# Splitting W_qkv's first two fifths inside the cross stage, and W_o with the first attention rows inside the self stage

## The reference

```python
x = x + cross_attention(layernorm(x), ctx_512)        # 16 heads over 1024 context rows
x = x + self_attention(layernorm(x))                  # w_qkv: 2560 x 512, 32 query heads, 4 key/value heads, causal
x = x + ffn(layernorm(x))                             # 16 experts, 4 chosen for a token, and a shared expert
...
qkv = jnp.einsum('bsh,oh->bso', hidden_states, w_qkv)
...
return jnp.einsum('bso,ho->bsh', out, w_o)            # w_o: 512 x 2048
```

## Time and profile before

| what | us |
|---|---|
| median of 3 runs | 1498.34 |
| lowest, highest | 1495.42, 1498.8 |
| the profiled execution | 1496.33 |
| its span, first to last instruction | 1494.4 |
| TensorE busy in it | 1355.5 |
| end of cross, start of self | 785 |
| end of self, start of MoE | 1059 |

### The profile page before, as it was taken

The page is one execution under the profiler, slowest core; times in us unless marked ns, Lnnn a source line. Parts: engine busy times, 40 slices in busy tenths (PEclk is TensorE's granted clock), DMA queues, the critical chain, the costliest instruction groups (busy, mean ns, idle before and its releaser), DMA issues. The chain is left out here.

```text
span 1494.4 us, 22780 instructions
## 1 busy us (share of the span) xinstructions
PE 1355.5 (91%) x7136; PEld 1109.7 (74%) x7136; DVE 800.7 (54%) x1371; ACT 737.9 (49%) x1741; POOL 573.0 (38%) x346
## 2 busy tenths in 40 slices
PE   5998699999999999999975999998689989999992
PEld 4776577878787878787854888887578768787772
DVE  4444366666666666666634445444479853432226
ACT  2444465565656565656524677777432214333331
POOL 2430133233332323232003333333346486427975
PEclk9999799999999999999997999999699999999997
DMA  5785414141414141413094111112643256536667
GB/s 195 262 269 178 172 50 149 54 173 50 175 49 175 48 177 43 182 42 113 1 330 178 64 64 50 50 50 99 225 146 132 78 184 225 174 121 224 233 201 232
DMA packets 78984, 209.79 MB, mean 140 GB/s; under 512 B 5888, under 2 KB 39168, under 8 KB 72960
## 3 DMA queue, kind: packets, MB, share of 16 engines
q1 hardware_dynamic: 69472, 163.78, 31.7%
q0 software_dynamic: 7136, 38.80, 7.6%
q10 hardware_dynamic: 2304, 6.29, 1.1%
HBM read 154.59 MB, written 92.01 MB: 165 GB/s over the span
## 5 line engine op out<-in xcount | busy, mean ns | idle before, releaser
L700 DVE TENSOR_TENSOR probsT_lo<-psTr,probsT_hi 128x512 fp32r<-128x512 f32 x256 | 176.7, 690 | 168.0 <-ACT probsT_hi L653 167.7
L653 ACT CAST probsT_hi<-psTr 128x512 fp32r<-128x512 f32 x256 | 150.1, 587 | 199.0 <-PE psTr L784 195.3
L784 PE MATMUL psTr<-ident,probs 128*128 128x128 f32 x1024 | 153.6, 274 | 11.3 <-DVE probsT_lo L700 5.2
L784 PEld LDWEIGHTS psTr<-ident,probs 128*128 128x128 f32 x1024 | 124.3, 141 | 50.4 <-DVE probsT_lo L700 13.5
L695 DVE TENSOR_REDUCE nmax<-psS 128x1 f32<-128x1024 f32 x128 | 155.5, 1215 | 9.5 <-PE psS L66 8.4
L610 ACT ACTIVATE probs<-psS,nmax 128x1024 f32<-128x1024 f32 x128 | 143.8, 1123 | 12.2 <-DVE nmax L695 12.2
L566 POOL TENSOR_TENSOR ctxT_lo<-ctx_f,ctxT_hi 128x512 fp32r<-128x512 f32 x32 | 41.4, 1295 | 278.0 <-ACT ctxT_hi L617 278.0
L64 PE MATMUL bank<-w_slots,ao_first_hi 128*128 (+1 forms) x252 | 108.5, 430 | 16.2 <-DVE w_slots L1807 9.6
L64 PE MATMUL psS<-kT_hi,qe 128*128 128x512 f32 x256 | 113.0, 441 | 3.7 <-DMA qe<-qe 2.8
L64 PE MATMUL psV<-probsT_hi,kv_hi 128*128 128x512 f32 x256 | 114.7, 448 | 0.6
L1513 POOL TENSOR_TENSOR w_slots<-w_ahead,w_slots 128x3072 fp32r<-128x3072 f32 x15 | 102.1, 6809 | 1.2
(11 more groups left out here) (273 smaller groups left out, 3323.8 us busy)
## 6 DMA issues: line engine op xcount, KB each, us to landing
w_ahead<-w_exp POOLq DMA_DIRECT2D x14, 1536.0 KB, 7.4
qe<-stage SPq DMA_DIRECT2D x16, 1024.0 KB, 6.8
qe<-qe SPq DMA_DIRECT2D x16, 1024.0 KB, 5.0
wraw<-w_pairs SPq DMA_DIRECT2D x8, 1792.0 KB, 11.5
early<-xs SPq DMA_DIRECT2D x47, 256.0 KB, 2.7
xs<-h_rows SPq DMA_DIRECT2D x47, 256.0 KB
early<-ctx SPq DMA_DIRECT2D x16, 512.0 KB, 11.6
ao<-attn_out SPq DMA_DIRECT2D x32, 256.0 KB, 2.4
```

The costliest lines, as they stand in the source:

```text
L653: act.copy(PT[k % PTN].hi[:], psT[slot][:]).then_inc(turned_hi, 1)
L700: dve.tensor_tensor(out, psT[slot][:], f32(hi), ALU.subtract).then_inc(turned_free, 1)
L784: last = pe.transpose(psT[slot][:, q * P:(q + 1) * P], src(q), ident[:])
```

## The change

**Memory.** One tensor `w_slots` is now allocated at the start for all blocks, and F, the queries, the keys, the context's parts, W_qkv, h2T, W_o and the first attention rows are views into it (`Shared`). Only by that can one block write into what the next one reads. Names in the lists change with it.

**In cross.** After its own work SyncE now also loads h2T for tiles 0 and 1, and, once a fifth is split, fifths 2 and 3 of W_qkv into the same two raw buffers. ScalarE casts fifth 0 after step k = 3 of the last half and fifth 1 after step k = 5 (`wqkv_high`), and waits there for the load; VectorE subtracts one step later (`wqkv_low`). The wait of ScalarE for the last two stores at the block's end is gone; it stands in later lists.

**In self.** The prologue has only fifths 2, 3 and 4 to split. W_o's quarters are loaded in units 2, 4, 6 and 7 of the first eight. In the last eight, GpSimd casts quarter c after its `norm` of unit c + 2, and VectorE subtracts it after its reciprocals of unit c + 3; in unit 6 GpSimd casts the first half of the attention rows, and in unit 7 VectorE subtracts them.

**In MoE.** The splits of W_o and of the first half-rows, the waits for them, and the load of the fourth quarter are gone. The second tile's first rows no longer wait for the first half of the projection.

```diff
+W_STEPS = (3, 5)
...
+        sp.wait_ge(pv_done, LT * (HB * NT - 1))
+        sp.wait_ge(h2_out, 16 * 3)
+        for j in range(2):
+            sp.dma_start(f32(HT[j]), h2_d[j].rearrange("p a x -> p (a x)")).then_inc(keep["ht_in"][j], 16)
+        for j in range(2):
+            sp.wait_ge(w_ready, j + 1)
+            sp.dma_start(keep["early"][j], t["w_qkv"][2 + j]).then_inc(w_in[2 + j], 16)
...
+        def wqkv_high(c):
+            act.wait_ge(s_mm, RT * HB * NT)
+            act.wait_ge(w_in[c], 16)
+            act.copy(W[c].hi, keep["early"][c]).then_inc(w_hi, 1)
...
+                    if not more and k in W_STEPS:
+                        wqkv_high(W_STEPS.index(k))
...
-        act.wait_ge(x1_out, 16 * NT + 16)
-        act.wait_ge(h2_out, 16 * NT + 16)
...
+        def wqkv_low(c):
+            dve.wait_ge(w_hi, c + 1)
+            dve.tensor_tensor(W[c].lo, keep["early"][c], f32(W[c].hi), ALU.subtract).then_inc(w_ready, 1)
...
+                    if not more and k - 1 in W_STEPS:
+                        wqkv_low(W_STEPS.index(k - 1))
...
+WO_SPLIT = (2, 3, 4, 5)
+WO_STEPS = (2, 4, 6, 7)
...
+            if isinstance(u, int) and u in WO_STEPS:
+                c = WO_STEPS.index(u)
+                if c == 0:
+                    sp.wait_ge(w_ready, WCH)
+                sp.dma_start(wo_raw[c], t["w_o"][:, c * KC:(c + 1) * KC, :]).then_inc(wo_in[c], 16)
...
+            if last and v in WO_SPLIT:
+                wo_high(WO_SPLIT.index(v))
+            if last and v == GI - 2:
+                pool.wait_ge(q_mm, NGRP)
+                pool.wait_ge(keep["a_in"][0], 16)
+                pool.tensor_copy(AS.hi, a_first).then_inc(wo_hi, 1)
...
-        high(0)
-        high(1)
+        high(2)
...
+            if last and v - 1 in WO_SPLIT:
+                c = WO_SPLIT.index(v - 1)
+                dve.wait_ge(wo_hi, c + 1)
+                dve.tensor_tensor(WO[c].lo, wo_raw[c], f32(WO[c].hi), ALU.subtract).then_inc(wo_lo, 1)
+            if last and v == GI - 1:
+                dve.wait_ge(wo_hi, HQ // 2 // KC + 1)
+                dve.tensor_tensor(AS.lo, a_first, f32(AS.hi), ALU.subtract).then_inc(wo_lo, 1)
...
-                if tt == 0 and h % KC == 0:
-                    pe.wait_ge(wo_lo, h // KC + 1)
```

More of the change, by code:

```diff
@@ L53 @@
 W_AHEAD = HQ * DH // P // KC - 1
+AT_QE, AT_KEYS = 0, 4 * H * S
+AT_F = AT_KEYS + 4 * L
+AT_KV = AT_F + 2 * H * D
+AT_CT = AT_KV + 4 * LT * DC
+WS_ALL = AT_CT + 2 * H * P
+WCH = 5
+WSZ = 2 * KC * BANK
+AT_A = 9 * KC * BANK
+HTZ, VBZ = 2 * KC * P, 8 * HKV * DH
+AT_CONST = WCH * WSZ
+AT_VB = AT_KV + 2 * HTZ
+AT_PT = AT_VB + 2 * VBZ
+assert AT_CONST + BANK + P <= AT_KV and AT_PT + 2 * REP * P <= WS_ALL
+assert 4 * W_B + 2 * T <= WS_ALL - AT_KV
 NE, TOPK, NG, TOPG, I = 16, 4, 4, 2, 256
@@ L77, in at, with __init__, shaped @@
         return self.hi[idx], self.lo[idx]
+class Shared(Pair):
+    def __init__(self, ws, at, dims):
+        n = int(np.prod(dims))
+        self.hi, self.lo = (shaped(ws[:, at + j * n:at + (j + 1) * n], dims) for j in range(2))
+def shaped(ap, dims):
+    names = "abcd"[:len(dims)]
+    return ap.rearrange(f"p ({' '.join(names)}) -> p {' '.join(names)}", **dict(zip(names, dims)))
 def f32(ap):
@@ L507, in tiles @@
         iteration(NT - 1, False, True)
+    W = [Shared(ws, c * WSZ, (KC, BANK)) for c in range(2)]
+    HT = [ws[:, AT_KV + j * HTZ:AT_KV + (j + 1) * HTZ] for j in range(2)]
+    w_in, w_hi, w_ready = keep["wqkv_in"], keep["wqkv_hi"], keep["wqkv_ready"]
     block = ctx.enter_context(nc.Block())
@@ L886, in sb @@
         return ctx.enter_context(nc.sbuf_tensor(name, shape, dt))
-    W = Pair(ctx, nc, "wqkv", [P, WCH, KC, BANK])
-    raw = keep["early"] + keep["ahead"][:WCH - 2]
+    ws = keep["ws"]
+    W = [Shared(ws, c * WSZ, (KC, BANK)) for c in range(WCH)]
+    a_first = keep["early_all"][:, 0:HQ // 4 * P].rearrange("p (h x) -> p h x", x=P)
+    raw = keep["early"] + keep["early"] + keep["ahead"][:1]
     tab = sb("rope_s_tab", [P, 2, 3, DH // 2])
-    mask_f, mask = sb("mask_f", [P, BANK]), sb("mask_r", [P, BANK], F32R)
-    ident_r = sb("ident_r", [P, P], F32R)
-    HT = [sb(f"h2T{j}", [P, 2, KC, P], F32R) for j in range(2)]
+    wo_raw = keep["ahead"] + [sb("wo_last", [P, KC, BANK])[:]]
+    WO = [Shared(ws, c * WSZ, (KC, D)) for c in range(HQ // 2 // KC)]
+    AS = Shared(ws, AT_A, (HQ // 4, P))
+    wo_hi, wo_lo = sem("wo_hi"), sem("wo_lo")
+    mask_f, mask = sb("mask_f", [P, BANK]), ws[:, AT_CONST:AT_CONST + BANK]
+    ident_r = ws[:, AT_CONST + BANK:AT_CONST + BANK + P]
+    HT = [shaped(ws[:, AT_KV + j * HTZ:AT_KV + (j + 1) * HTZ], (2, KC, P)) for j in range(2)]
     QR = sb("q_terms", [P, 2, BANK])
@@ L960, in _ @@
     def _(sp):
-        sp.dma_start(HT[0][:].bitcast(F32).rearrange("p a k x -> p a (k x)"), t["h2T"][0]).then_inc(ht_in[0], 16)
         sp.dma_start(tab[:], t["rope_s"]).then_inc(tab_in, 16)
         sp.dma_start(mask_f[:], t["mask"]).then_inc(tab_in, 16)
[L964 to L970, removed]
+        sp.dma_start(raw[4], t["w_qkv"][4]).then_inc(w_in[4], 16)
         def step(i, v, last):
             u, tt, g, ahead = plan(i, v, last)
+            if isinstance(u, int) and u in WO_STEPS:
[3 more added lines that the diff above has]
+                sp.dma_start(wo_raw[c], t["w_o"][:, c * KC:(c + 1) * KC, :]).then_inc(wo_in[c], 16)
             if last and v == 2:
@@ L1098, in step @@
                 exps(u + 1, (v + 1) % 2)
+            if isinstance(u, int) and u == 1:
+                act.wait_ge(keep["h2_out"], 16 * NT + 16)
             if not (isinstance(u, int) and u == 0):
@@ L1147, in v_low @@
                                       ALU.subtract).then_inc(v_lo, 1)
[L1149 to L1150 removed]
+        low(2)
         dve.wait_ge(tab_in, 32)
@@ L1153, in _ @@
         terms_q(0)
-        low(2)
+        low(3)
         terms_q(1)
-        low(3)
+        dve.wait_ge(keep["x1_out"], 16 * NT + 16)
         maxes(0, 0)
@@ L1331, in build_moe @@
     acc = sb("acc", [P, NT, D])
-    WS = sb("w_slots", [P, (NSLOT - 1) * SLOT + 2 * KC * T], F32R)
+    WS = keep["ws"]
     h3 = [WS[:, (NSLOT - 1) * SLOT + j * KC * T:(NSLOT - 1) * SLOT + (j + 1) * KC * T].rearrange(
```

110 lines of the change are left out of this document (52 added, 58 removed).

## The result

| what | before | after |
|---|---|---|
| median of 4 runs each, us | 1497.57 | 1515.04 |
| lowest, highest | 1495.42, 1498.8 | 1513.6, 1519.25 |
| the profiled execution | 1496.33 | 1515.2 |
| its span | 1494.4 | 1513.2 |

The ratio is 1.0117, its 95% interval 1.0099 to 1.0135: the change makes the kernel 17.5 us slower. The forecast was +19.1, and 1517.4 us counted from the median of 1498.34 that three runs had; a fourth has joined them.

What follows compares the result with a forecast made beforehand. TensorE, busy 91% of the span, was taken as the bound, so only its waits count. +19.2 (first keys) - 1.5 (prologue) + 1.4 (W_o) = +19.1 us, giving 1517.4 us; range 1507 to 1525, slower 93%.

Steps and rivals of the forecast that it cites:

- fifth 0 in the raw buffer, ScalarE's cast starts: End of cross: fifth 0 of W_qkv, queued behind 8 MB of fills, lands at 779 (776 to 781); ScalarE waits.
- step 4's cast later by: Last half of cross: step 4 is cast at 780.9 instead of 757.54, +23.4 us.
- rest of the half: Cross after ScalarE's wait: second cast, subtractions and TensorE's slow clock add +3.1 us, between 1 and 6.
- TensorE's first keys later by: Start of self: TensorE starts its keys at about 808.6 instead of 789.36, +19.2 us.
- prologue, to the first unit: Start of self: one meeting of VectorE's subtraction with GpSimd's `q_rope` goes away, -1.5 us (0 to -2.2).
- collisions in the last units: Last units of self: W_o subtractions behind the reciprocals block GpSimd's `norm` four times, +7.1 us (3 to 9).
- start of MoE: MoE's first projection: with everything already split, TensorE can begin at once, -5.7 us.
- TensorE's start of MoE later by: Sum of all forecast terms up to TensorE's first MoE projection: +19.1 us.
- The arrival: End of cross: fifth 0 of W_qkv lands at 779, taken from between 778 and 780.3.
- the moved store: End of cross: h2T's 0.5 MB store now stands behind ScalarE's second new cast, giving back up to 1.7 us.
- The rival in which the clock stays low for the rest of cross: Cross after the stop: TensorE may stay at 1.2 GHz, +8 instead of +3, kernel at 1523; chance 13%.
- what the block's end gave back: End of cross: the block ends some 0.6 us after the last h2T store's issue, instead of 3.8 us.

Runs made afterwards that it cites:

- experiments with fewer fills: Changed kernel with two of SyncE's four zero fills ahead of the W_qkv loads: 1503.79 us; with none ahead: 1491.0 us.
- loads first: Kernel before the change, with the loads of the first two W_qkv fifths moved ahead of the four zero fills: 1501.02 us; same edit in the changed kernel: 1491.0.
- fills in self: Four zero fills moved from the end of cross into units 1, 3, 5, 7: kernel before 1500.16 us, changed kernel 1491.47, version with shorter prologue 1481.2.
- subtraction ahead of the reciprocals: Changed kernel with VectorE subtracting each W_o quarter before its unit's reciprocals instead of behind them: 1510.07 us.
- two fills: Changed kernel with two of the four zero fills ahead of the W_qkv loads and two behind them: 1503.79 us.

## Why the prediction was right, step by step

| step | predicted | measured |
|---|---|---|
| fifth 0 in the raw buffer, ScalarE's cast starts | 779 | 778.38 |
| step 4's cast later by | 23.4 | 22.65 |
| rest of the half | 3.1 | 1.4 |
| TensorE's first keys later by | 19.2 | 17.0 |
| prologue, to the first unit | -1.5 | -2.2 |
| units up to the last eight | 0 | +0.9 |
| collisions in the last units | +7.1 | +6.8 |
| start of MoE | -5.7 | -6.1 |
| TensorE's start of MoE later by | 19.1 | 16.4 |
| the whole kernel | 19.1 | 17.5 (profiled 18.8) |

**The arrival** was the step that decided the sign. It was read from two rows of the kernel before, the issue time and the 30.8 us to landing, and held within 0.6 us; fifth 0 took 29.1 us (749.29 to 778.38), 1.7 less, as much as the sum allowed at most for the moved store. The experiments with fewer fills showed that the arrival is the cause.

**The rest of the half** was mis-sized: 1.4 us instead of 3.1. The granted clock came back sooner than in the earlier trace rows. TensorE began at 781.55 with matmuls of 0.78 and 0.63 us and was at 0.40 by 785.83, 4 us instead of 6, and the second cast (783.18) and the subtractions found gaps. The table by stretch shows the same (granted clock, DMA share and GB/s last):

```profile
782.00:784.00 2.00, 2.00 (x8) 1.71 (x7) 2.00 (x2) 1.30 (x2) 0.00 (x0) 0.50 0.26 104
784.00:786.00 2.00, 2.00 (x9) 1.56 (x9) 0.29 (x1) 1.29 (x2) 0.00 (x0) 0.68 1.05 309
786.00:788.00 2.00, 2.00 (x12) 1.65 (x12) 1.59 (x2) 0.76 (x2) 0.00 (x0) 1.00 0.96 377
```

The level of 1.2 GHz (0.50) is left between 784 and 786. The rival in which the clock stays low for the rest of cross did not come.

**The prologue**: one `q_rope` of 3.24 us at 814.89 and one of 1.26 at 825.22 stand where the earlier trace rows had 3.24 twice (the second of them not shown), as forecast. TensorE was at full clock from 809.04 on, 2.7 us into its keys, which is probably where the 0.7 us more than taken come from; no run isolates it.

**The last units**: four `norm` of 2.98 instead of 1.04, each 1.9 us longer; 3.2 was forecast for each. The Trainium skill's exclusive lock ("SBUF — State Buffer", "SBUF: two separate sides") is what the trace shows: the loser ends about 0.9 us after the winner. Moving the subtraction in the list took all of it away. From the reciprocals ahead of the first of them (1047.95, 15.7 us later than before) to TensorE's last `psO` (1077.51, 22.6 later) that makes 6.8 us. Quarter 0, still covered by queries, cost 0.6 (0.8 was taken), and the three others 2.3, 1.9 and 1.9, together 6.2 (6.3 was taken).

**Two steps weren't in the sum.** The units in the middle of self took 0.9 us more; no run isolates why. And from TensorE's start of MoE to the end of the span it took 431.8 us instead of 429.4. These 2.4 us can't be put down to the change: two experiments that leave the MoE block of the kernel before as it is took 434.7 us there (loads first) and 433.6 (fills in self), and those with the MoE block of the changed kernel took 429.6 (subtraction ahead of the reciprocals) to 435.3 (two fills). Executions with the same MoE lists differ by more than that.

**Part of the closeness is luck.** Up to the start of MoE the forecast was 2.7 us too high, 19.1 against 16.4: 0.8 in the arrival, 1.7 in the rest of the half, 0.7 in the prologue and 0.7 in the last two steps, less the 0.9 us of the middle units and 0.2 in what the block's end gave back. The whole kernel came nearer, to within 1.6 us by the medians and 0.3 by the profiled executions, because more time went by after that point than before the change, and no step of the forecast has that. The mechanism and the sign don't hang on that.

## What to carry to other kernels

Moving work to an earlier place in an engine's list moves its wait for data with it, and everything queued behind. Ask of each moved step when its data lands, in the trace of the kernel before, and what stands ahead of the load in its queue, before counting what the old wait cost. And where a heavy VectorE instruction is moved next to an event that also starts GpSimd, try the other side of the event, or halves of the instruction.

## What the runs showed that wasn't expected

- **A full queue slows a store in another one.** ScalarE's 0.5 MB store took 2.7 us alone and 20.0 to 21.8 us beside SyncE's fills of 2 MB each. This was 0.1 us from mattering in the kernel before, and mattered as soon as anything shifted.
- **A gain of a microsecond can turn into a loss** where two engines meet: which of two instructions 0.16 us apart goes first decided 2 us of `q_rope` and 3 us of TensorE's wait, and the two kernels with the fills in self lost their earlier start by it in the same way.
- **A wait put down to "issue"** (7.54 us at the first unit) was an ordinary wait for VectorE's list; a new order of that list and of ScalarE's shortened it to 1.45.
